# Graph attention on one Trainium2 core: places of the sums kept in registers, and a group's logits in one piece

## The reference

```python
msg = xl[src] + xr[dst]
act = jnp.where(msg > 0, msg, NEG_SLOPE * msg)
e = jnp.einsum('ehd,hd->eh', act, att)
m = jax.ops.segment_max(e, dst, num_segments=n)
p = jnp.exp(e - m[dst])
denom = jax.ops.segment_sum(p, dst, num_segments=n)
alpha = p / (denom[dst] + 1e-16)
out = jax.ops.segment_sum(alpha[..., None] * xl[src], dst, num_segments=n)
```

## Time and profile before

| | |
|---|---|
| runs, median of 3 (lowest to highest) | 2544.92 us (2539.33 to 2546.8) |
| profiled execution, its own time | 2550.99 us |
| its span, first to last instruction | 2549.2 us |
| PE busy | 1907.4 us, 75% |
| DVE busy | 1588.1 us, 62% |
| ACT busy | 1186.7 us, 47% |
| POOL busy | 1060.3 us, 42% |
| products L2009 of the fused stage | first 1477.2, last 2399.1 us |

### The profile page before, as it was taken

The page is one execution under the profiler, slowest core; times in us unless marked ns, Lnnn a source line. Parts: engine busy times, 40 slices in busy tenths (PEclk is TensorE's granted clock), DMA queues, the critical chain, the costliest instruction groups (busy, mean ns, idle before and its releaser), DMA issues. The chain is left out here.

```text
span 2549.2 us, 51811 instructions
## 1 busy us (share of the span) xinstructions
PE 1907.4 (75%) x12291; PEld 1205.4 (47%) x12291; DVE 1588.1 (62%) x4358; ACT 1186.7 (47%) x4251; POOL 1060.3 (42%) x1564
## 2 busy tenths in 40 slices
PE   4899999867776767777589826777777677667778
PEld 3555555435554545545377613444444444444443
DVE  6677777655555555555599715655656565657768
ACT  3100000246566656666476503555545454546666
POOL 1122222156666666666211172444545454545140
PEclk9999999979999999999799957778888887888779
DMA  8344433068888888888799643434434343434447
GB/s 314 104 103 110 109 101 98 32 216 290 290 283 294 285 290 288 286 292 284 225 334 323 203 133 94 110 100 109 110 107 111 96 113 98 113 98 109 90 149 265
DMA packets 209851, 456.26 MB, mean 179 GB/s; under 512 B 41915, under 2 KB 111288, under 8 KB 209648
## 3 DMA queue, kind: packets, MB, share of 16 engines
q0 software_dynamic: 90000, 281.90, 34.5%
q1 hardware_dynamic: 89008, 144.64, 18.8%
q10 hardware_dynamic: 30672, 27.93, 4.9%
HBM read 419.97 MB, written 47.44 MB: 183 GB/s over the span
## 5 line engine op out<-in xcount | busy, mean ns | idle before, releaser
L161 POOL DMA_INDIRECT ring<-xl_table,isrc x440 | 444.2, 1010 | 463.9 <-DVE w L2115 217.6
L1270 ACT ACTIVATE wone<-onehot,w 128x64 f32<-128x64 f32 x1760 | 434.7, 334 | 288.3 <-DVE onehot L1316 166.9
L1287 PE MATMUL banks<-w_sb,wone 128*64 128x256 f32 x2368 | 341.5, 409 | 139.8 <-DVE acc L1312 55.1
L161 POOL DMA_INDIRECT w_sb<-xp_table,isrc x296 | 297.6, 1006 | 173.4 <-PE banks L1290 92.6
L1887 PE MATMUL banks<-acc 64*128 64x264 f32 x880 | 197.2, 530 | 194.5 <-ACT lg L1829 78.7
L995 PE MATMUL banks<-w_sb,acc 128*128 128x512 f32 x736 | 342.1, 604 | 0.0
L1845 ACT ACTIVATE w<-ring,pw 128x64 f32<-128x64 f32 x1320 | 325.4, 334 | 0.0
L2009 DVE SCALAR_TENSOR_TENSOR acc<-banks,w 128x512 f32<-128x512 f32 x220 | 145.9, 688 | 287.0 <-remote 182.9
L1892 PE MATMUL banks<-ring,ident 128*128 128x260 f32 x880 | 307.6, 479 | 2.2 <-issue 2.1
L1312 DVE TENSOR_TENSOR acc<-banks,acc 128x512 f32 x440 | 304.4, 692 | 0.0
L1311 DVE TENSOR_TENSOR zacc<-banks,zacc 64x9 f32 x440 | 69.5, 158 | 330.9 <-PE banks L1290 194.6
(11 more groups left out here) (338 smaller groups left out, 2938.9 us busy)
## 6 DMA issues: line engine op xcount, KB each, us to landing
acc<-xr_table SPq DMA_DIRECT2D x440, 66.0 KB
lt_bc<-local_dst ACTq DMA_DIRECT2D x110, 128.0 KB, 3.6
w<-acc SPq DMA_DIRECT2D x100, 128.0 KB, 4.7
x_table<-y POOLq DMA_DIRECT2D x25, 512.0 KB, 7.7
acc<-x_table SPq DMA_DIRECT2D x25, 512.0 KB, 3.6
low_bc<-src_low ACTq DMA_DIRECT2D x98, 128.0 KB, 4.2
acc<-in_x SPq DMA_DIRECT2D x12, 1024.0 KB, 13.3
xp_table<-xp_st SPq DMA_DIRECT2D x24, 512.0 KB
```

Of the source, the lines that this page charges most:

```text
L161: return self.pool.indirect_dma_start(out, None, table, bass.IndirectOffsetOnAxis(ap=idx, axis=0), bounds_check=self.bound, oob_is_err=False)
L1270: last = nc.scalar.activation(wone[:, s, j, h, :], onehot[:, s, j, :], ACT.Copy, scale=w9[:, bass.ds(g * U + j, 1), h:h + 1].rearrange("p ...
L1287: nc.tensor.matmul(psum[WN * a:WN * (a + 1), j, k * C:(k + 1) * C], wone[:, s, j, h, :], slots[r][:, j, h * C:(h + 1) * C], start=True, st ...
```

## The change

It has two parts, both in the fused stage.

*Places in registers.* The moves from a tile's window to the next one's (0 or 1; 439 of them and a 0) are packed once on DVE, 20 to a word, into 22 words (`pack_moves`, in the first group of block 1), and these are loaded into 22 registers. DVE keeps the current window in the register `place`. After each addition `go_on` takes the lowest bit of the block's word, adds it to `place` and shifts the word. So that the loop can use the same registers in each turn, the words are moved down by RU = 3 registers at the end of each turn. The load of 4 words a group is gone from DVE; SP keeps its own.

*Logits in one piece.* PE computes all 4 tiles in a row (four products with the one-hots in the order 0, 2, 1, 3, then four with the identity), waits for product and copy of the whole group before, and signals once. The product is one instruction over 4 banks, and so is ACT's copy. All waits on `s_pg`, `s_pd` and `s_sc` count groups instead of halves.

```diff
--- before.py
+++ after.py
@@ -1713,13 +1713,15 @@
             au = sb("au6", [TB, 2, NB])
             auh = sb("auh6", [TB, 2, NB, H])
             edge = sb("edge6", [P, 2])
+            packed_i = sb("packed6", [P, NBLK], I32)[32:33, :]
+            moves, packed = between.take(T)[32:33], between.take(NBLK)[32:33]
             upper = sb("upper6", [P, 1])
             s_lt = [sem(f"q_lt{i}") for i in range(3)]
             s_xr = [sem(f"q_xr{i}") for i in range(BG)]
             s_mk = [sem(f"q_mask{i}") for i in range(3)]
             s_r = [sem(f"q_r{i}") for i in range(RG)]
-            (s_first, s_edge, s_const, s_zero, s_ab, s_ot, s_pg, s_sc, s_pd, s_pt, s_lg, s_au0, s_au, s_aut, s_any) = (
-                sem("q_" + n) for n in "first edge const zero ab ot pg sc pd pt lg au0 au aut any".split())
+            (s_first, s_edge, s_const, s_zero, s_ab, s_ot, s_pg, s_sc, s_pd, s_pt, s_lg, s_au0, s_au, s_aut, s_any, s_pack) = (
+                sem("q_" + n) for n in "first edge const zero ab ot pg sc pd pt lg au0 au aut any pack".split())
             (s_t1, s_sl, s_ck, s_fb, s_t2, s_c, s_fd, s_fe, s_t3, s_m, s_f, s_ff, s_e, s_t4, s_wv, s_ws) = (
                 sem("b_" + n) for n in "t1 sl ck fb t2 c fd fe t3 m f ff e t4 wv ws".split())
             s_o, s_sm, s_wa, s_wd, s_mm, s_rs, s_acc = (sem("r_" + n) for n in "o sm wa wd mm rs acc".split())
@@ -1767,7 +1769,7 @@
                               .then_inc(s_lt[r], 16)
 
                     def load_near(g, i, at):
-                        wait(sp, s_pg, 2 * (g - BG + 1))
+                        wait(sp, s_pg, g - BG + 1)
                         for j in range(U):
                             half = slice(WN * (j // 2), WN * (j // 2 + 1))
                             sp.dma_start(near[half, i, j % 2, :], xr_w[bass.ds(at[j], 1)].rearrange("w n c -> (w n) c"))\
@@ -1815,7 +1817,7 @@
                         ahead = (BG * r + i) // BG
                         slot, at, s = ahead % RU, i % BG, (BG * r + i) % 3
                         act.wait_ge(s_lt[slot], 32 * m + 32 * (ahead // RU) + 32)
-                        wait(act, s_pg, 2 * (g - 2))
+                        wait(act, s_pg, g - 2)
                         away = onehot_t[:, s].rearrange("p q e -> p (q e)")
                         nc.scalar.activation(away, lt[:, slot, at, :], ACT.Abs, bias=edge[:, 0:1]).then_inc(s_ab, 1)
                         act.wait_ge(s_ab, g + 1)
@@ -1824,10 +1826,9 @@
                     onehots(1, 0, 1, 0)
 
                     def self_logits(g, r, i):
-                        for e in range(2):
-                            act.wait_ge(s_pd, 2 * g + e + 1)
-                            nc.scalar.activation(lg[:, r, :, i * U + e:(i + 1) * U:2].rearrange("p n j -> p j n"),
-                                                 psum[:, 2 * e:2 * e + 2, HID:XRW], ACT.Copy).then_inc(s_sc, 1)
+                        act.wait_ge(s_pd, g + 1)
+                        nc.scalar.activation(lg[:, r, :, i * U:(i + 1) * U].rearrange("p n j -> p j n"),
+                                             psum[:, 0:U, HID:XRW], ACT.Copy).then_inc(s_sc, 1)
 
                     def weigh(u, r, k, i):
                         g, rg, on, r2, i2 = steps_of(u, r, k, i, BACK - 1)
@@ -1879,18 +1880,17 @@
                         rg = BG * r + i
                         pe.wait_ge(s_ot, g + 1)
                         pe.wait_ge(s_xr[i], 64 * (RU * m) + 64 * r + 64)
-                        for e in range(2):
-                            wait(pe, s_pd, 2 * (g - 1) + e + 1)
-                            wait(pe, s_sc, 2 * (g - 1) + e + 1)
-                            for j in (e, e + 2):
-                                half = slice(WN * (j // 2), WN * (j // 2 + 1))
-                                nc.tensor.matmul(psum[:, 2 * e + j // 2, 0:XRW], onehot_t[half, rg % 3, j % 2, :],
-                                                 near[half, i, j % 2, :], start=True, stop=False)
-                            if e == 0:
-                                pe.wait_ge(s_r[rg], 16 * U * m + 16 * U)
-                            for j in (e, e + 2):
-                                last = nc.tensor.matmul(psum[:, 2 * e + j // 2, 0:XLW], ident[:], ring[:, rg * U + j, :], start=False, stop=True)
-                            last.then_inc(s_pg, 1)
+                        wait(pe, s_pd, g)
+                        wait(pe, s_sc, g)
+                        for j in (0, 2, 1, 3):
+                            half = slice(WN * (j // 2), WN * (j // 2 + 1))
+                            nc.tensor.matmul(psum[:, j, 0:XRW], onehot_t[half, rg % 3, j % 2, :],
+                                             near[half, i, j % 2, :],
+                                             start=True, stop=False)
+                        pe.wait_ge(s_r[rg], 16 * U * m + 16 * U)
+                        for j in range(U):
+                            last = nc.tensor.matmul(psum[:, j, 0:XLW], ident[:], ring[:, rg * U + j, :], start=False, stop=True)
+                        last.then_inc(s_pg, 1)
 
                     def borders():
                         pe.wait_ge(s_au, 1)
@@ -1967,7 +1967,27 @@
 
                 @block.vector
                 def _(dve):
-                    windows = StepTiles(dve, wtab, "r1", U, NW)
+                    words = [dve.alloc_register(f"r1_word{b}") for b in range(NBLK)]
+                    place = dve.alloc_register("r1_place")
+                    moved = dve.alloc_register("r1_moved")
+                    dve.reg_mov(place, 0)
+
+                    def pack_moves():
+                        link = Chain(dve, s_pack)
+                        link(nc.vector.memset(moves[:, T - 1:T], 0.0))
+                        link(nc.vector.tensor_tensor(moves[:, 0:T - 1], wtab[:, 1:T], wtab[:, 0:T - 1], ALU.subtract))
+                        by_block = moves.rearrange("p (b s) -> p b s", s=BS)
+                        link(nc.vector.tensor_copy(packed, by_block[:, :, BS - 1]))
+                        for s in reversed(range(BS - 1)):
+                            link(nc.vector.scalar_tensor_tensor(out=packed, in0=packed, scalar=2.0, in1=by_block[:, :, s],
+                                                                op0=ALU.mult, op1=ALU.add))
+                        link(nc.vector.tensor_copy(packed_i, packed))
+
+                    def go_on(word):
+                        dve.reg_alu(moved, word, 1, ALU.bitwise_and)
+                        dve.reg_alu(place, place, moved, ALU.add)
+                        dve.reg_alu(word, word, 1, ALU.logical_shift_right)
+
                     consts = Chain(dve, s_edge)
                     consts(nc.vector.tensor_scalar(upper[:], pidx[:], WN - 0.5, float(WN), ALU.is_gt, ALU.mult))
                     nc.vector.tensor_tensor(edge[:, 0:1], upper[:], pidx[:], ALU.subtract)
@@ -2003,23 +2023,22 @@
                         dve.wait_ge(s_zero, 4)
 
                     def product(g):
+                        dve.wait_ge(s_pg, g + 1)
                         wait(dve, s_pt, g)
-                        for e in range(2):
-                            dve.wait_ge(s_pg, 2 * g + e + 1)
-                            nc.vector.scalar_tensor_tensor(out=prod[:, 2 * e:2 * e + 2], in0=psum[:, 2 * e:2 * e + 2, 0:HID], scalar=0.0,
-                                                           in1=bc(att_relu[:].unsqueeze(1), [P, 2, HID]),
-                                                           op0=ALU.max, op1=ALU.mult).then_inc(s_pd, 1)
+                        nc.vector.scalar_tensor_tensor(out=prod[:], in0=psum[:, 0:U, 0:HID], scalar=0.0,
+                                                       in1=bc(att_relu[:].unsqueeze(1), [P, U, HID]),
+                                                       op0=ALU.max, op1=ALU.mult).then_inc(s_pd, 1)
 
                     def reduce(g):
-                        dve.wait_ge(s_pd, 2 * g + 2)
+                        dve.wait_ge(s_pd, g + 1)
                         nc.vector.tensor_reduce(out=part[:], in_=prod[:].rearrange("p j (h c) -> p j h c", h=H),
                                                 op=ALU.add, axis=AX.X).then_inc(s_pt, 1)
 
                     def finish(g, r, i):
                         dve.wait_ge(s_pt, g + 1)
-                        dve.wait_ge(s_sc, 2 * g + 2)
-                        v = lg[:, r, 0:H, i * U:(i + 1) * U].rearrange("p h (a e) -> p e a h", e=2)
-                        nc.vector.tensor_tensor(v, v, part[:].rearrange("p (e a) h -> p e a h", e=2), ALU.add).then_inc(s_lg, 1)
+                        dve.wait_ge(s_sc, g + 1)
+                        v = lg[:, r, 0:H, i * U:(i + 1) * U].rearrange("p h j -> p j h")
+                        nc.vector.tensor_tensor(v, v, part[:], ALU.add).then_inc(s_lg, 1)
 
                     def scan_step(u, r, k, i, m):
                         r1 = (r - 1) % RU
@@ -2078,7 +2097,8 @@
```

(26 more changed lines are left out.)

## The result

The changed kernel is slower: 2568.73 us median (2558.53 to 2586.51, 4 runs) against 2543.15 (2539.33 to 2546.8, 4 runs), a ratio of 1.0089 with a 95% interval of 1.0052 to 1.0127. The forecast was 2544 us, no change; 2568.73 lies inside its range, but the interval leaves no room for "no change". The profiled execution has a span of 2560.4 us for 2549.2.

A forecast was written before the change was run, and what follows sets the result against it. The prediction took waits, chiefly PE's signals held during POOL's gather runs, to bound the kernel. Its terms, -6.6 - 11.5 + 7.5 + 7 + 5 - 2.5, summed to -1.1 us, giving 2544 us, no change, range 2514 to 2574.

The forecast's parts named there:

- What bounds the kernel: Fused stage's loop: no engine is full; waits set the pace, with PE's signals reaching DVE late during POOL's gather runs.
- Term 1: Loop groups: the register load leaves DVE, three register operations behind each addition replace it; 6.6 us saved (0 to 12).
- Term 2: About 23 held loop groups: the single signal goes when the first half's did; 11.5 us saved (or lost).
- rival (a): Held groups: the single signal is held until the old second release; 2567 us, chance 0.16.
- Term 3: One handshake a group instead of two: longer chain of product, ACT and PE; 7.5 us lost (2 to 25).
- rival (b): Loop: the chain product, ACT, PE, product becomes the bound, 0.25 us a group more; 2566 us, chance 0.11.
- Term 4: Opening of the stage: packing the moves once on DVE and loading 22 words; 7 us lost (4 to 9).
- Term 5: Loop's turns: 18 register copies lose 5 us; a gap partly vanishing under the longer product saves 2.5 us.
- rival (d): Loop: POOL's rhythm sets the pace, so the load's gain and half the held groups' gain vanish; 2556 us, chance 0.06.

The follow-up runs named there:

- e17: Kernel before with places in registers, halves kept, packing in group 1, and only the first 60 tiles gathered: 2319.13 us, ratio 0.9118.
- e1: Kernel before with only the places in registers, logits still in halves: ratio 0.9988.
- e3: Changed kernel with the packing and the load of 22 words moved early, to group 1: ratio 1.0008.
- e4: Changed kernel run once more, unaltered, on the same chip as its parts: ratio 1.0057.
- e6: Kernel before with places in registers, halves kept, and the packing early in group 1: ratio 0.9934.
- e13: Changed kernel with early packing, PE signalling after tile 1 and tile 3, and DVE's product in halves again: ratio 0.996.
- e18: e6 with POOL's opening run of 60 gathers broken up by waits for earlier products: 2519.86 us, ratio 0.9903 to the kernel before.
- e2: Kernel before with only the logits in one piece, windows still loaded four words a group: ratio 1.0033.
- e5: Kernel before, unaltered, run again for one more profile: 692.3 us from group 15 to 100.
- e7: Kernel before with PE signalling once a group, behind its second half; two products kept: ratio 1.0101.
- e8: Kernel before with PE waiting for both halves of the group before; two signals and two products kept: ratio 0.9987.
- e14: Kernel before with only the first 60 tiles gathered and the ring's rows used again: 2308.37 us, ratio 0.9136.
- e15: Kernel before with one PE signal a group, two products, and only the first 60 tiles gathered: 2322.37 us, ratio 0.9191.
- e16: Changed kernel with only the first 60 tiles gathered: 2345.62 us, ratio 0.9283 to the kernel before.
- e11: e6 rerun in the third set; its intended unused 4-word load was dropped when built: ratio 1.0044 to the kernel before.

## Why the prediction was wrong

**What bounds the kernel** was read rightly: without the runs of gathers the loop takes 499 us for 692 to 712, and no remote wait is left.

**Term 1** (-6.6 us). 0 (498.4 against 498.7). The load's 0.27 us is gone, as forecast: an unheld product waits for nothing, and e17's waits for issue fell from 36.4 to 16.4 us. But the register operations were taken at 0.12 us where their upper bound, 0.27, was the right end. With the gathers something stands there that the prediction had at nothing: all seven profiles of versions with places in which signals are held (the changed kernel's, e1, e3, e4, e6, e13, e18) have 12 to 18 waits for issue before the weigh, up to 1.9 us long, 7.0 to 16.2 us together (the 15.1 above), and before, e2, e5, e7 and e8 have none. In one of them DVE's sequencer took 0.71 us over a register operation that takes 0.08 otherwise.

**Term 2** (-11.5 us) took the single signal to be let go when the first of the two was, and priced the other case at 0.5 us a group. Counted in the timelines of the loop, of the waits over 0.6 us before a product those that ended only some 2.2 us behind the start of the run's last gather were 2 of 30 for the first half before (14 us together), none of 31 in e5, but 9 of 35 for the single signal of the changed kernel (66 us) and 16 of 46 in e7 (103 us), most of some 7 us each. That is rival (a)'s mechanism, and its ground is plain afterwards: PE gave the first signal 1.7 us sooner, before or early in the run. What it costs on the whole isn't settled. e7 costs 25 us with gathers and 14 without, so about 11 us are the hold's in it (some 4 to 20 by e7's interval, and e14 and e15 have two runs each). But e7 isn't the change: the changed kernel costs less with the gathers than without, and e2, which has the single signal as well, only 8 us (1.0033). No run shows the gain of 11.5 us as such. The Trainium skill (TensorE: Matmul & The Clock Gate, "The cost: per-tile semaphore tail") says that a single increment on the last matmul saves time; here it costs 1.0% (e7), as what waited for the first of the two starts later.

**Term 3** (+7.5 us) is the step that failed, by its size: 12.0 us in the loop by the signal alone and 18.7 with the whole change where 3.5 were forecast, 6 to 8 in the opening (e2, e3) for 4. I compared when the *last* result comes, 4.6 us against 4.75. But before, DVE needed only the *first* half to go on, some 1.7 us earlier, and that slack covered the groups with little other work. The chain I had also begins too late: behind the weigh PE first does the sums (1.12 us). The upper bound, 25 us, held it. This is rival (b)'s mechanism at rival (b)'s price: 18.7 us over 85 groups are 0.22 us each (0.25 forecast), though they fall on one group of five, and mostly where PE runs at 1.2 GHz, as it said. Its sign, a growing wait of the product for L1892, shows only without the gathers (8.3 to 31.2 us; with them 28.5 and 26.4). That its 2566 us come so close to 2568.73 is luck, as it keeps the gains of terms 1 and 2.

**Term 4** (+7 us): 7.4 on DVE, and the first product behind it 2.1 us later than the others, because PE's clock fell meanwhile; e2 to e4 have 7.4 us in the opening, e5 to e1 10.0. The load of 22 words lasted 1.84 us in the trace (0.084 a word, 0.074 taken); the Trainium skill (Runtime: NRT & Kernel Launch, "Instruction fetch mechanics") has about 200 ns a register, 4.4 us, and the trace contradicts it again.

**Term 5** (+5 - 2.5): 0. In e14, e17 and e16 the longest wait at a turn is 3.4 us, with and without the 18 copies; they run inside the gap that was there, and the gap is no shorter.

**The sum** of the stretches in the profiles without gathers is 120.8 - 107.3 for the opening, 26.9 - 29.6 for groups 10 to 15, 18.7, and 52.1 - 49.9 for the end: 31.7 us (the medians differ by 37). With the gathers the change costs 14 to 23 us by the two ratios. So where signals are held, part of the loss doesn't count. That a group which waits for POOL's end doesn't care for a later result would explain it, as rival (d) said of the gains, but no run shows it group by group. Had terms 1, 3 and 5 been put at what these runs show (0, 25 to 27 and 0 us), the forecast would have been a loss of 20 to 22 us, even with terms 2 and 4 as they stood.

**Open.** The places take 0.66% off with the gathers (e6) and nothing without them. e1, less its 7 to 10 us of packing, points the same way. What differs must be how the steps fall into POOL's runs; no run shows which step, and I don't settle it. Nor is it shown what the single signal's longer holds cost the changed kernel: a version of it with and without an early signal, in one set and both with and without the gathers, wasn't run.

## What to carry to other kernels

A signal in the middle of a batch of work isn't only bookkeeping: before merging two, ask what the waiting engine does between the first and the second, above all in the step where it has least other work. One-time work belongs where the engine waits anyway: the same packing cost nothing some forty microseconds earlier (e6), though it took 18 us there for 7.4. And if a loop is ruled by chance, take the cause of the chance out (here the gathers) and price each edit there, as single profiles of it differ by more than the edits do.

## What the runs showed of the hardware

- POOL's gathers held signals in four of the five sets and in the first runs, and not in the third set. There the kernel before took 2124 us, elsewhere 2522 to 2545. In the third set e11, with all its gathers, has no remote wait in the loop and takes 499.5 us from group 15 to 100; its gathers take 1026 ns each, those of e6 1014. The cut of the gathers changes nothing there (0.9989) and 8.6% in the fourth set (0.9136). What makes the difference isn't known, nor whether it is the chip's.
- DVE's waits for its own signals get longer as well in a long run of gathers. In e3, under the opening's run, the packing's chained instructions of 0.19 us go at 0.23 us each at first, and then at 1.40 to 1.46 us each, while POOL issues a gather each 1.31 us. In the changed kernel, where no gather is running, all of them go at 0.23 (19 in 4.27 us):

```profile
1513.33 2.52 DVE L1982 SCALAR_TENSOR_TENSOR acc<-acc 1x22 f32<-1x22 f32 x11
1516.22 0.19 DVE L1982 SCALAR_TENSOR_TENSOR acc<-acc 1x22 f32<-1x22 f32 x1 [0.38 <-issue]
1517.62 0.19 DVE L1982 SCALAR_TENSOR_TENSOR acc<-acc 1x22 f32<-1x22 f32 x1 [1.21 <-DVE acc L1982]
1519.02 0.19 DVE L1982 SCALAR_TENSOR_TENSOR acc<-acc 1x22 f32<-1x22 f32 x1 [1.21 <-DVE acc L1982]
```

- 18 register copies ahead of a loop's branch cost nothing that shows beside a gap of 3.2 to 3.4 us that the turn has anyway (e14, e17).
